# Which engine splits the MLP weight slabs, how far ahead they are loaded, and where one store stands in the DMA queue

## The reference

```python
x   = layer_norm(hidden, ln1_w, ln1_b)
q, k, v = x @ q_w + q_b, ctx @ k_w + k_b, ctx @ v_w + v_b      # 16 heads of 32
attn = softmax(where(mask, q @ k.T / sqrt(32), min))
hidden = attn @ v @ cproj_w + cproj_b + hidden
y   = gelu(layer_norm(hidden, ln2_w, ln2_b) @ fc_w + fc_b)     # width 2048
out = hidden + y @ proj_w + proj_b
```

## Time and profile before

| what | before |
|---|---|
| median of the runs | 793.99 us |
| the profiled execution | 793.99 us |
| its span, first to last instruction | 792.2 us |
| PE busy | 750.8 us (95%) |
| DVE / ACT / POOL busy | 466.1 / 276.1 / 290.8 us |
| mean granted TensorE clock | 0.996 |

### The profile page before, as it was taken

How to read it: one execution, slowest core, us unless ns; L and a number is a source line. 1 busy time by engine, 2 the same in 40 slices (tenths; PEclk the granted TensorE clock), 3 DMA queues, 4 the chain that set the end, 5 groups by cost and what they waited for, 6 DMA issues and landing times.

```text
span 792.2 us, 10041 instructions
## 1 busy us (share of the span) xinstructions
PE 750.8 (95%) x3664; PEld 516.0 (65%) x3664; DVE 466.1 (59%) x1008; ACT 276.1 (35%) x489; POOL 290.8 (37%) x171
## 2 busy tenths in 40 slices
PE   7999999889999998999999997899999999999998
PEld 5878886633344343344437885688888888888886
DVE  5674337789888889898766655543423434232213
ACT  4434241366756556565782111021112111111111
POOL 2644040066886667997665001122002200120000
PEclk9999999999999999999999999899999999999999
DMA  8647286696764684698333334412130403030001
GB/s 319 234 153 246 112 251 204 212 273 156 186 151 122 160 225 116 156 223 199 85 132 107 120 94 132 146 62 98 27 79 1 160 13 71 24 106 1 1 0 54
DMA packets 94385, 103.25 MB, mean 130 GB/s; under 512 B 39968, under 2 KB 48420, under 8 KB 94336
## 3 DMA queue, kind: packets, MB, share of 16 engines
q1 hardware_dynamic: 94192, 102.59, 45.1%
q10 hardware_dynamic: 144, 0.02, 0.0%
HBM read 73.08 MB, written 29.37 MB: 129 GB/s over the span
## 4 chain that ended last, share of the span: by engine, by line
PE 80%; DVE 12%; ACT 3%; issue 2%; DMA 2%; SPq 1%; POOL 0%; DVEq 0%
PE ps L471 21%; PE ps L473 20%; PE ps L472 20%; DVE ps L975 6%; PE ps L578 6%; PE ps L594 5%; PE ps L609 3%; PE ps L563 3%; ACT Pt L771 3%; DMA RW<-in_proj_w 1%; DVE R L913 1%; PE ps L531 1%; DVE mx L975 1%; SPq L331 1%; DVE BIG L1006 1%
## 5 line engine op out<-in xcount | busy, mean ns | idle before, releaser
L771 ACT ACTIVATE Pt<-ps 128x512 f32<-128x512 f32 x256 | 134.3, 603 | 84.5 <-PE ps L578 84.5
L1135 DVE CAST HR<-R 128x512 fp32r<-128x512 f32 x52 | 25.1, 482 | 182.7 <-ACT R L804 182.5
L804 ACT ACTIVATE R<-ps,cols 128x512 f32<-128x512 f32 x52 | 35.9, 690 | 235.7 <-PE ps L473 235.7
L578 PE MATMUL ps<-BIG 98*128 98x512 f32 x256 | 92.3, 438 | 13.0 <-ACT Pt L771 11.2
L578 PEld LDWEIGHTS ps<-BIG 98*128 98x128 f32 x256 | 44.3, 188 | 82.1 <-ACT Pt L771 37.8
L975 DVE CUSTOM_DVE_ANT_0 ps<-ps,FU 128x512 f32<-128x512 f32 x128 | 84.5, 721 | 17.3 <-PE ps L563 17.3
L975 DVE CUSTOM_DVE_ANT_0 ps<-ps,BIG 128x512 f32<-128x512 f32 x128 | 84.5, 722 | 16.4 <-PE ps L563 16.3
L471 PE MATMUL ps<-BIG,HR 128*128 128x512 f32 x192 | 74.9, 390 | 2.3 <-DVE HR L1137 2.3
L471 PE MATMUL ps<-YT,BIG 128*128 128x512 f32 x192 | 75.0, 390 | 0.0
L472 PE MATMUL ps<-YT,BIG 128*128 128x512 f32 x192 | 74.7, 389 | 0.0
L472 PE MATMUL ps<-BIG,HR 128*128 128x512 f32 x192 | 74.7, 389 | 0.0
(11 more groups left out here) (125 smaller groups left out, 1389.3 us busy)
## 6 DMA issues: line engine op xcount, KB each, us to landing
BIG<-qs SPq DMA_DIRECT2D x62, 256.0 KB, 2.8
BIG<-ks SPq DMA_DIRECT2D x62, 256.0 KB, 3.2
ks<-BIG SPq DMA_DIRECT2D x32, 256.0 KB, 2.0
qs<-BIG SPq DMA_DIRECT2D x32, 256.0 KB, 5.6
R<-hd SPq DMA_DIRECT2D x28, 256.0 KB, 3.8
R<-in_x SPq DMA_DIRECT2D x16, 256.0 KB, 5.0
hd<-R SPq DMA_DIRECT2D x16, 256.0 KB, 2.1
yt<-FU SPq DMA_DIRECT2D x64, 64.0 KB, 1.9
```

The source lines that it names most:

```text
L578: eng.matmul(bk, K_[0:98, j, kc * 128:(kc + 1) * 128], Q_[0:98, j, :], start=True, stop=True).then_inc(S["p_ra"], 1)
L771: eng.activation(Pt[:, r, j % 2, :], bank(bank_a(("s2", i, j))), ACT.Exp, scale=SCALE).then_inc(S["a_ra"], 1)
L804: eng.activation(g, bank(4 + i % 2), ACT.Gelu_apprx_tanh, bias=fcb[:, f:f + 1]).then_inc(S["a_g"], 1)
L1135: eng.tensor_copy(HR[:, n, 0, :], g).then_inc(S["v_hh"], 1)
```

## The change

1. `s1` group 7 and its maxima move one Q projection later (`EARLY_Q`).
2. SP stores `LAST_Q` with the other Q stores, ahead of the load of `cproj_w`, and not in loop step 2.
3. Pair adds: DVE keeps the second half of pairs 28, 30 and 31 only; POOL does the other five halves of pairs 28 to 31.
4. Slab low parts: slabs 0 to 4 are DVE's, slabs 5 to 15 are POOL's. Slab 0 is split in steps 56 and 57, and the loads run one step further ahead (`load_slab(i+5)`).
5. The affine, high and low parts of batch 0's layer norm are moved by up to two steps.
6. The four adds of L1292 for batch 0 are all in MLP step 8.

```diff
-        EARLY_K, EARLY_Q = {0: 3, 1: 4, 2: 5}, {0: 6, 1: 7}
+        EARLY_K, EARLY_Q = {0: 3, 1: 4, 2: 5}, {0: 6, 2: 7}
-        Y_BLOCKS, Y_AFFINE, Y_HIGH, Y_LOW = (41, 45, 46, 49), (56, 56, 56, 56), (56, 56, 57, 57), (57, 57, 58, 58)
+        Y_BLOCKS, Y_AFFINE, Y_HIGH, Y_LOW = (41, 45, 46, 49), (56, 56, 57, 57), (57, 57, 58, 58), (58, 58, 60, 60)
         def added(i, hp):
             m = i // 2
-            return ("g_ac", 2 * m + hp + 1) if m < BY_DVE else ("v_ac", 2 * (m - BY_DVE) + hp + 1)
+            if hp and m in BY_DVE:
+                return "v_ac", BY_DVE.index(m) + 1
+            return "g_ac", 2 * m + hp + 1 - sum(n < m for n in BY_DVE)
         def lows(f):
-            return ("g_sl", 2 * f + 2) if f < 3 else ("v_sl", 2 * f - 4)
+            return ("v_sl", 2 * f + 2) if f < 5 else ("g_sl", 2 * f - 8)
-        BY_DVE = 28
-        SLAB_HIGH, SLAB_LOW = (58, 59, 62), (59, 60, 63)
+        BY_DVE = (28, 30, 31)
+        SLAB_HIGH, SLAB_LOW = (56, 59, 62), (57, 60, NI)
     # SP, before the loop
-                    if (b, g) != LAST_Q:
-                        store_qk(b, g, 1)
+                    store_qk(b, g, 1)
     # SP, loop
                 if i == 2:
-                    store_qk(*LAST_Q, 1)
                     for n in range(1, 4):
                         load_mask(n)
             load_slab(4)
+            load_slab(5)
     # SP, MLP
-                if 1 <= i < 12:
-                    load_slab(i + 4)
+                if 1 <= i < 11:
+                    load_slab(i + 5)
     # DVE, loop
-                if kc % 2 and i // 2 >= BY_DVE:
-                    pair_add(i, 0)
...
-                if kc % 2 and i // 2 >= BY_DVE:
-                    pair_add(i, 1)
+                if i in SLAB_LOW:
+                    slab_low(SLAB_LOW.index(i))
+                if kc % 2 and i // 2 in BY_DVE:
+                    r = (2 * i + 1) % 6
+                    dve.wait_ge("a_ra", RA[("s2", i, 3)] + 1)
+                    dve.wait_ge("p_sm", (i // 2 - 3) // 2 + 1)
+                    eng.tensor_tensor(pair(i // 2)[:, 2:4, :], Pt[:, (r - 2) % 6, :, :], Pt[:, r, :, :], ALU.add)...
     # DVE, MLP
                     divide_c(NS - 1)
+                    slab_low(2)
+                    slab_high(3)
+                    slab_low(3)
-                for f2 in range(3, NF):
-                    if i == (1 if f2 == 3 else 2 if f2 == 4 else 13 if f2 == 15 else f2 - 3):
-                        slab_high(f2)
-                        slab_low(f2)
+                if 1 <= i < 12:
+                    slab_high(i + 3)
+                if i == 1:
+                    slab_low(4)
+                if i == 13:
+                    slab_high(15)
     # POOL, loop
-                if i in SLAB_LOW:
-                    slab_low(SLAB_LOW.index(i))
-                if kc % 2 and i // 2 < BY_DVE:
-                    for hp in range(2):
+                if kc % 2:
+                    for hp in range(1 if i // 2 in BY_DVE else 2):
     # POOL, MLP
-                for c in range(4):
-                    if f == (8 + c if b == 0 else 3):
+                if 2 <= i < 12:
+                    slab_low(i + 3)
+                if i == 13:
+                    slab_low(15)
+                if f == (8 if b == 0 else 3):
+                    for c in range(4):
```

More of the change, by code:

```diff
@@ L994, in divide_c @@
                 eng.tensor_tensor(prod(s), R1[:, 0, :], R1[:, 2, :], ALU.mult).then_inc(S["v_at"], 1)
[L996 to L1000, removed]
             def slab_low(f):
@@ L1004, in slab_low @@
                 for h in range(2):
-                    dve.wait_ge("v_sh", 2 * f + h - 5)
+                    if f < 3:
+                        dve.wait_ge("a_sh", 2 * f + h + 1)
+                    else:
+                        dve.wait_ge("v_sh", 2 * f + h - 5)
                     eng.tensor_tensor(sl[2 * h + 1], RW[:, f % 2, 512 * h:512 * h + 512], sl[2 * h].bitcast(F32),
@@ L1120, in _ @@
                         y_affine(0, k)
-                if kc % 2 and i // 2 >= BY_DVE:
-                    pair_add(i, 1)
+                if i in SLAB_LOW:
[4 more added lines that the diff above has]
+                    dve.wait_ge("p_sm", (i // 2 - 3) // 2 + 1)
+                    eng.tensor_tensor(pair(i // 2)[:, 2:4, :], Pt[:, (r - 2) % 6, :, :], Pt[:, r, :, :], ALU.add).then_inc(S["v_ac"], 1)
             for i in range(NJ + 1):
@@ L1209, in slab_low @@
                 for h in range(2):
-                    pool.wait_ge("a_sh", 2 * f + h + 1)
+                    pool.wait_ge("v_sh", 2 * f + h - 5)
                     low(sl[2 * h + 1], RW[:, f % 2, 512 * h:512 * h + 512], sl[2 * h], "g_sl")
```

## The result

The changed kernel takes 802.47 us (median of 4 runs, 801.44 to 804.0), the kernel before 793.91 us (793.81 to 795.04) on the same chip: a ratio of 1.0106, 95% interval 1.0088 to 1.0125. It is slower, by 8.6 us, and lies above the forecast's range (788.5 to 800.5). The kernel before spread from 791 to 797 us on the chips of the later experiments, so each of them is compared with its own runs of before.

What follows compares the result with a forecast made beforehand. The prediction took PE, busy for 95% of the span, as the bound. Its terms, 7.15 + 2.0 + 2.9 + 0.4 - 10.85 = +1.6 us on 793.99, gave 795.6 us, range 788.5 to 800.5.

Steps and rivals of the forecast that it cites:

- edits 1 and 2, front: Start of attention loop: late maxima 0.7 us, PE waits for two rows of maxima 2.7 and 3.75; 7.15 us, bounds 0.7 to 9.
- step 57: Late attention loop: DVE and POOL alternate, divide_a(13) comes late and s2(59, 0) waits; +2.0 us, bounds 0 to 2.5.
- HR(1): First MLP steps: added DVE work alternating with POOL makes HR of step 1 late for pj(1); +2.9 us.
- MLP's hole: MLP at 480 to 503 us: two PE idle times and the slow clock go; -10.85 us.
- `fc(12)`: MLP step 8: POOL's four adds wait for loads, so the low part this needs is late; +0.4 us (0 to 2).
- Rival B: The clock falls in the new PE idle times, costing 2 to 3 us; 798.6 us, chance 0.20.
- the three idle times of 2.7 us and more: New PE waits: 2.7 and 3.75 us for rows of maxima at the front, 2.9 us ahead of pj(1).
- rival C: MLP: POOL bounds the slabs, fc waits in several steps, half of the 10.85 us is lost; 801 us, chance 0.10.
- The two rows of maxima: Attention loop front: small stores land behind the 1 MB load, at 171.5 and 190.1; PE waits 2.7 and 3.75 us.
- A: Front: the queue is no obstacle, maxima land in time, edits 1 and 2 cost 0.7 us; 789.1 us, chance 0.20.
- D: Neither DVE-POOL alternation, at 392 and 427 us, reaches PE; 790.7 us, chance 0.08.
- The two alternations: DVE and POOL waiting for each other's whole instructions at 392 and 427 us; +2.0 and +2.9 us.

Runs made afterwards that it cites:

- e6: Changed kernel plus matmuls that nobody reads, put where PE waits for the maxima at the front; 800.02 us, ratio 1.0072.
- e12: e6 run again for a second trace; 797.32 us (one run).
- e3: Changed kernel with edits 1 and 2 undone; 791.7 us, ratio 0.9962.
- e7: e3 with POOL's four adds of L1292 in MLP step 11 in place of 8; 788.04 us, ratio 0.993.
- e10: e3 with the four adds in MLP step 11, the first low part in step 58 and slab 3 split behind HR(1); 782.97 us, ratio 0.9872.
- e5: Kernel before with edit 1 alone; 795.95 us, ratio 1.0026.
- e2: Changed kernel with edit 1 undone; 799.31 us, ratio 1.0069.
- e4: Kernel before with edit 2 alone; 803.9 us, ratio 1.0118.
- e14: Kernel before, unchanged, run again for a second trace; 793.85 us (one run).
- e9: e3 with slab 0's low part on DVE moved from loop step 57 to 58; 789.68 us, ratio 0.9955.
- e11: e3 with POOL's two adds of x moved from MLP step 1 to step 2, behind slab_low(5); 786.82 us, ratio 0.9916.
- e13: Changed kernel, unaltered, run again for a second trace; 800.46 us (one run).
- e1: Changed kernel with edit 2 undone; 794.09 us, ratio 0.9998.

## Why the prediction was wrong in size

The steps; "clean" is a trace without a slow clock at the place, and the last column has the two traces of the changed kernel.

| step | predicted | measured, clean | in the changed kernel |
|---|---|---|---|
| edits 1 and 2, front | +7.15 | +7.0, +7.4 (e6, e12) | +13.4, +9.3 |
| step 57 | +2.0 | +1.6 (e3) | +1.6, +1.6 |
| HR(1) | +2.9 | +2.7 (e7) | +2.6, +4.2 |
| MLP's hole | -10.85 | -11.15 (e7, e10) | not by itself |
| `fc(12)` | +0.4 | +2.6 (e3 less e7) | PE's wait: 2.5, 2.3 |
| gelu 3 to the end, hole and `fc(12)` together | -10.45 | -8.6 (e3) | -6.8, -8.6 |

The prediction had the change slower, and for the reasons that the traces show; the size was off.

**The step that failed is the sum of edits 1 and 2, 7.15 us, where the changed kernel's traces have 13.4 and 9.3, both above its bound of 9.** It took every duration of the front at the full clock. As a sum of transfers and waits it was right: with matmuls in the waits the front costs 7.0 us and the second row lands at 190.4 where 190.1 was written. In the changed kernel the clock falls behind the 2.1 us wait at 153, and again in the waits for the maxima. The first fall makes step 1, and so the stores on SP's list, later (165.21 against 163.27), and the rows behind them with it; the later falls lengthen the steps that follow (from step 8 to step 10 the shift grows from 10.8 to 13.7 us, in e6 it doesn't grow). Rival B had this mechanism, with chance 0.20 and a price of 3 us; as an addition to the front, with what the queue's own scatter adds, it measured 6.2 and 2.1 us in two traces. It looked for the fall in the three idle times of 2.7 us and more. The first one, of edit 1, was not among them: the prediction had DVE's wait of 2.0 us and the late start of `s1(8)`, 0.7 us, but didn't say that PE would be idle over the same 2 us. e5 shows this part by itself: the 2.1 us wait and the slow clock cost 2.4 us in the trace, 1.5 us in the medians.

The prediction's argument for B used one number, that PE had been idle for 3.6 us before the fall of the earlier trace rows. But before had also idled 2.32 us at 484 without one, and after 2.12 us at 153 the clock did fall. The length of the idle time alone doesn't decide it. Nor does the work just ahead of it: e2 and before give PE the same matmuls and the same wait here, and the clock falls in e2 only. First PE's wait and the clock in e2, then in before:
```profile
153.55 0.50 PE L579 MATMUL ps<-BIG 98*128 98x512 f32 x1 [1.33 <-DVE BIG L963]
...
154.00:156.00 2.00, 2.00 (x10) 1.44 (x9) 1.37 (x5) 0.74 (x2) 0.00 (x0) 0.72 0.48 178
```
```profile
153.50 0.50 PE L578 MATMUL ps<-BIG 98*128 98x512 f32 x1 [1.33 <-DVE BIG L962]
...
154.00:156.00 2.00, 2.00 (x12) 1.45 (x12) 1.42 (x5) 0.74 (x2) 0.00 (x0) 1.00 0.74 250
```
A full fall that gives 0.72 comes 1.1 us before the stretch's end, at 154.9. Nor does it fall there in e3, e4 and e14, which have that wait too. What sets e2 apart is not known; a single trace can't say of a short gap that it is safe. The Trainium skill ("TensorE: Matmul & The Clock Gate", "Why this matters for your kernels") advises to keep PE's idle gaps between bursts of matmuls under a length that is longer than 2.12 us. The clock fell here behind 2.12 and behind 1.33 us, so this case doesn't bear that length out as a safe bound.

**The second term that was off is `fc(12)`, 0.4 us (0 to 2), where PE waited 2.5.** The loads of the four adds were issued from 498.67 and released POOL at 503.97, 5.3 us later, where the sum had 3.6. The adds took 5.18 us, and `slab_low(12)` was late by 2.5 us. This is rival C's mechanism in one step only, not in several.

**What held.** The two rows of maxima wait behind the big load (A is refuted: they land 7.8 and 15.1 us after their issue). The two alternations reach PE (D is refuted): e9 takes the first away, and e11 brings the second from 2.4 to 0.3 us. The rule of the Trainium skill ("SBUF — State Buffer", "Who interferes with whom"), an exclusive lock between the two engines' shared ports, agrees with 1.29 against 3.47 us for the same two subtractions: a halved bandwidth would make 2.6. Edits 4 and 6 remove both idle times at 484 to 503, and the slow clock there.

The first trace's own sum is 13.4 + 1.6 + 2.6 - 11.15 + 2.5 = 9.0 us, and its span is longer by 803.1 - 792.2 = 10.9. The 1.9 us between them I put to the slow clock at 514. e13 bears this out: the same kernel, without that fall, makes -8.6 us of the stretch from gelu 3 to the end, against -6.8 in the first trace. Its own sum, 9.3 + 1.6 + 4.2 - 11.15 + 2.3 = 6.3, is near its 6.5 us.

**What stays open.** How much of the median of 8.6 us is the clock. The first trace of the changed kernel less that of e6 gives 6.5 us for the front, e13 less the mean of e6 and e12 gives 2.1, and the medians (800.0 and 802.5) give 2.5 with intervals that overlap. In all of these the scatter of the queue's landings is included, so 2 to 6.5 us is a range for both together. No run has the slab loads one step further ahead without the low parts on POOL, so it isn't shown which of the two gives the 11.15 us. Also not tried: edit 2 with the maxima's rows on another queue, which would separate the order on SP from the bytes.

## What to carry to other kernels

A store that waits for compute, put ahead of a large load on one queue, delays everything listed behind it, and small transfers that gate the next step pay for it (10.6 us in e4). To list those before the load is the remedy to try; no run here did. Price a new idle time of PE with the clock it may cost and with what the slower PE then feeds back to the queue, not with its length alone, and take that price from more than one trace. When moving work from DVE to POOL, look at which DVE instruction waits next on the critical path: the transfer, together with the earlier loads, gained 11 us where DVE was late for want of a slab, and lost 1.6 and 2.6 us where both engines met ahead of an instruction that PE waits for. With those two meetings and the four adds put right, and edits 1 and 2 left out, the kernel is 1.3% faster than before (e10).

## What the runs showed of the hardware

The same program shows different falls of the clock from run to run: twice or three times in the front of the changed kernel, whose front costs 9.3 or 13.4 us. Behind the same 2.1 us wait near 153 us the clock stayed at its lower level for 3.4 us in the first trace of the changed kernel, 6.8 in e5 and in e13, and 10.2 in e1. An 8 KB transfer took 6.4 us to land behind 1.5 MB and 15.1 us behind the queue of the changed kernel, and 13.4 us in e6. Beside POOL, DVE's instructions that read only SBUF took longer: the pair L1004 from 1.29 to 3.48 us and the cast from 0.41 to 1.49 us, whereas an add with one operand in PSUM (L1100), with POOL's pair add running from 404.38 to 406.78, kept the 0.69 us that such an add takes elsewhere:
```profile
404.98 0.69 DVE L1100 TENSOR_TENSOR R<-ps,R 128x512 f32<-128x512 f32 x1 [2.40 <-PE ps L474]
```
